# A gated cross-attention and ternary feed-forward kernel: 16-bit projections in a new order on every engine

## The reference

```python
q = heads(layernorm(x) @ Wq); k = heads(context @ Wk); v = heads(context @ Wv)
attn = softmax(where(mask, q @ k.T * 16 ** -0.5, -max))
x = x + tanh(g_xattn) * (merge(attn @ v) @ Wo)
h = gelu(layernorm(x) @ ternary(W1).T + b1)
x = x + tanh(g_ffn) * (h @ ternary(W2).T + b2)
```

## Time and profile before

| | |
|---|---|
| median of 3 runs | 1667.67 us (1663.63 to 1668.81) |
| profiled execution | 1664.17 us, its span 1662.4 us |
| busy in the span | PE 91%, DVE 90%, ACT 57%, POOL 40% |
| the chain that ended last | PE 55%, DVE 26%, issue 13%, ACT 3% |
| granted TensorE clock, mean | 0.984 of full |

### The profile page before, as it was taken

How to read it: one execution, slowest core, us unless ns; L and a number is a source line. 1 busy time by engine, 2 the same in 40 slices (tenths; PEclk the granted TensorE clock), 3 DMA queues, 4 the chain that set the end, 5 groups by cost and what they waited for, 6 DMA issues and landing times.

```text
span 1662.4 us, 48262 instructions
## 1 busy us (share of the span) xinstructions
PE 1508.0 (91%) x14501; PEld 1007.7 (61%) x14501; DVE 1489.1 (90%) x4379; ACT 939.8 (57%) x1799; POOL 668.8 (40%) x813
## 2 busy tenths in 40 slices
PE   3899999999999999999999999987999999999998
PEld 2566666666666666666666666655666666666665
DVE  7799999999999999999999999987888888888886
ACT  2456666665656666565656566654555555555554
POOL 5354555455555545554555545552111111111111
PEclk9899999999999999999999999996999999999999
DMA  2333333333333333333333333321010110101101
GB/s 78 92 99 85 96 84 88 93 86 97 84 96 83 97 84 94 86 87 95 86 97 83 98 83 95 81 49 55 26 38 25 38 38 25 38 25 38 38 25 51
DMA packets 207471, 117.93 MB, mean 71 GB/s; under 512 B 24912, under 2 KB 207184, under 8 KB 207440
## 3 DMA queue, kind: packets, MB, share of 16 engines
q1 hardware_dynamic: 207440, 117.54, 26.2%
HBM read 32.53 MB, written 16.78 MB: 30 GB/s over the span
## 4 chain that ended last, share of the span: by engine, by line
PE 55%; DVE 26%; issue 13%; ACT 3%; DVEq 2%; ACTq 0%; DMA 0%
PE bank L1069 12%; PE bank L312 9%; PE bank L1098 5%; PE bank L1099 5%; DVE smax L751 5%; PE bank L336 5%; PE bank L319 4%; PE bank L303 4%; DVE rstd L691 3%; DVE xres L796 3%; DVE k L721 3%; PE bank L392 2%; DVE rstd L693 2%; DVE y L1056 2%; DVE rstd L684 2%
## 5 line engine op out<-in xcount | busy, mean ns | idle before, releaser
L924 POOL TENSOR_TENSOR probl<-prob 128x512 f16<-128x512 f32 x512 | 529.2, 1042 | 531.2 <-ACT prob L602 530.3
L602 ACT ACTIVATE prob<-bank,masks 128x512 f32<-128x512 f32 x512 | 345.4, 688 | 138.9 <-PE bank L371 138.9
L751 DVE TENSOR_REDUCE smax<-bank 128x4 f32<-128x512 f32 x512 | 348.2, 681 | 13.5 <-PE bank L336 9.7
L1085 DVE TENSOR_TENSOR hidl<-hid 128x512 f16<-128x512 f32 x256 | 226.0, 883 | 80.5 <-ACT hid L1080 79.7
L1080 ACT ACTIVATE hid<-bank,b_sb 128x512 f32<-128x512 f32 x256 | 176.1, 688 | 211.3 <-PE bank L1069 205.3
L1069 PE MATMUL bank<-y,w1T 128*128 128x512 f16 x1024 | 264.6, 381 | 29.2 <-DVE y L1056 28.0
L1163 POOL TENSOR_TENSOR xres<-xres,b2g 128x1024 f32 (+1 forms) x32 | 75.7, 2366 | 431.4 <-ACT yln L1033 413.5
L1098 PE MATMUL bank<-w2T,hid 128*128 128x256 f16 x1024 | 237.4, 273 | 0.6 <-ACT w2T L1013 0.6
L1099 PE MATMUL bank<-w2T,hidl 128*128 128x256 f16 x1024 | 237.4, 273 | 0.0
L336 PE MATMUL bank<-k_rows,q_rows 64*128 64x128 f16 x2048 | 226.8, 220 | 5.6 <-DMA q_rows<-smaxT 3.4
L371 PE MATMUL bank<-q_rows,k_rows 64*128 64x128 f16 x2048 | 201.7, 219 | 0.8 <-DMA q_rows<-smaxT 0.8
(11 more groups left out here) (92 smaller groups left out, 2555.7 us busy)
## 6 DMA issues: line engine op xcount, KB each, us to landing
q_rows<-q SPq DMA_DIRECT2D x512, 64.0 KB, 2.5
k_rows<-k SPq DMA_DIRECT2D x512, 64.0 KB, 2.5
xres<-in_x_dram SPq DMA_DIRECT2D x64, 256.0 KB, 2.7
out_dram<-ystage SPq DMA_DIRECT2D x32, 512.0 KB, 2.9
ctx_sb<-in_ctx_dram SPq DMA_DIRECT2D x64, 192.0 KB, 3.2
q_rows<-smaxT SPq DMA_DIRECT2D x128, 8.0 KB
w_raw<-in_L_ffn_W_dram SPq DMA_DIRECT2D x2, 1024.0 KB, 7.0
prob<-in_L_xattn_Wq_dram SPq DMA_DIRECT2D x1, 256.0 KB, 4.2
```

Source lines behind the costliest of these rows:

```text
L602: act.activation(prob[u][:], st_bank[u % 2][:], ACT.Exp, bias=0.0, scale=masks[g.parity][:, 2 + b:3 + b]).then_inc(exp_done, 1)
L751: dve.tensor_reduce(smax[:, b, u * UH:(u + 1) * UH], sm_bank[u % 2][:].rearrange("p (h j) -> p h j", h=UH), AX.X, ALU.max).then_inc(max_ta ...
L924: pool.tensor_tensor(probl[u][:], prob[u][:], prob[u][:].bitcast(BF16)[:, 1::2], ALU.subtract).then_inc(prob_split, 1)
```

## The change

It has six parts.

1. The four weight matrices are scaled by 64 and split into two float16 parts at the start (ACT's `high_weights`, DVE's `low_weights`). Each float32 matmul of a projection becomes three 16-bit ones: high by high, high by low, low by high (`SPLIT`). The scale is taken off where q and k are split, through the gate for the output, and through the constant `vone` for v.
2. `xln` and the context are split before they are transposed. POOL's `low_x` and `low_ctx` write the float16 rest into the lower half of each float32 word in place, and PE transposes both halves as 16-bit tiles (8 transposes of 128x128 in place of 4, for each of the two). `low_prob` writes in place, too: `probl` is gone, and the low part is read with a step of two.
3. The attention result of both batches is transposed at once (4 float32 transposes), split (ACT `copy_attnT`, DVE `low_attn`), projected at once (12 matmuls) and added at once (one `add_attention` of 128x512).
4. The layer norm's statistics are taken once for four batches. In the loop DVE does only the first four parts (`seed_x`), and the Newton steps go to POOL (`root_x`, 14 parts over seven units). `load_x` loads four batches at once.
5. `read_weighed` writes its sums back to PSUM, from where `normalise` reads them. `low_q` and `low_k` are one instruction of 128x512 each, and k has two buffers.
6. All five lists are in a new order. The rough scores run one unit further ahead.

```diff
         def project_q(pe, g, m):
...
             for k in range(KD):
-                last = pe.matmul(pj_bank[:, m * T:(m + 1) * T], wq_sb[:, k, m * P:(m + 1) * P],
-                                 xlnT[:, k, :], start=(k == 0), stop=(k == KD - 1))
+                for i, (wp, xp) in enumerate(SPLIT):
+                    last = pe.matmul(by_batch(m), wq16[:, wp, k, m * P:(m + 1) * P],
+                                     typed(xT16[:, xp, k, :], xp).rearrange("p (b s) -> p b s", b=2),
...
         def read_weighed(dve, n, b, half):
...
-            dve.tensor_reduce(attn[b][:, heads, :],
-                              pv[:, :, 0:2 * HD].rearrange("p h (two d) -> p h d two", two=2), AX.X,
-                              ALU.add).then_inc(norm_read, 1)
+            dve.tensor_reduce(sums_of(half), pv[:, :, 0:2 * HD].rearrange("p h (two d) -> p h d two", two=2), AX.X,
+                              ALU.add).then_inc(sums_taken, 1)
...
-            dve.tensor_tensor(attn[b][:, heads, :], attn[b][:, heads, :],
+            dve.tensor_tensor(attn[b][:, heads, :], sums_of(half),
                               rsum[:, b, heads].unsqueeze(2).to_broadcast([P, HB, HD]),
...
+        def low_x(pool, g):
+            pool.wait_ge(ln_done, 2 * (g.n + 1))
+            x = xln[:].rearrange("p b d -> p (b d)")
+            pool.tensor_tensor(x.bitcast(F16)[:, 0::2], x, x.bitcast(BF16)[:, 1::2], ALU.subtract).then_inc(x_split, 1)
...
+        def low_attn(dve, g):
+            dve.wait_ge(attnT_high, g.n + 1)
+            dve.tensor_tensor(attnT16[:, 1].rearrange("p k t -> p (k t)"), tr_bank[:],
+                              attnT16[:, 0].rearrange("p k t -> p (k t)"), ALU.subtract).then_inc(attnT_split, 1)
...
         def low_prob(pool, g, b, u):
...
-            pool.tensor_tensor(probl[u][:], prob[u][:], prob[u][:].bitcast(BF16)[:, 1::2],
+            pool.tensor_tensor(prob[u][:].bitcast(F16)[:, 0::2], prob[u][:], prob[u][:].bitcast(BF16)[:, 1::2],
                                ALU.subtract).then_inc(prob_split, 1)
...
         def pool_group(pool, g, left):
             for b in range(2):
                 for u in range(UNITS):
                     low_prob(pool, g, b, u)
-                    if b == 1 and u == 0 and left >= 1:
+                    k = b * UNITS + u
+                    if g.parity == 1 and left >= 6 and k >= 4:
+                        for i in range(2 * k - 8, 2 * k - 6):
+                            root_x(pool, g.half + 3, i)
+                    if g.parity == 0 and left >= 4 and k < 3:
+                        for i in range(2 * k + 8, 2 * k + 10):
+                            root_x(pool, g.half + 2, i)
+                    if k == 3 and left >= 3:
+                        low_x(pool, g.after(3))
+                    if k == 4 and left >= 1:
                         pick_masks(pool, g.after(1))
+                    if k == 6 and left >= 3:
+                        low_ctx(pool, g.after(3))
```

More of the change, by code:

```diff
@@ L451, in pe_first @@
             transpose_max(pe, g0, 0, tr)
-            for u in range(2):
+            for u in range(3):
                 rough_scores(pe, g0, 1, u)
@@ L694, in ln_part @@
             else:
[L695 removed]
+                last = dve.scalar_tensor_tensor(norm[:, 0, :] if i == LN_PARTS - 2 else y, t, 1.5, y, ALU.add,
+                                                ALU.mult)
             last.then_inc(step, 1)
@@ new lines, in seed_x @@
+        def seed_x(dve, half, i):
+            past = half - 2
+            if i == 0:
+                dve.wait_ge(x_in, 16 * (half + 1))
+                for b in range(QB):
+                    last = dve.bn_stats(stats[:, b, :], row_of(half * QB + b))
+            elif i == 1:
+                if not (isinstance(half, int) and half == 2):
+                    dve.wait_ge(ln_ready, half)
+                dve.wait_ge(seed_step, past * (SEED_PARTS - 1) + 1)
+                dve.tensor_copy(rstd[:, 2, :], stats[:, :, 1])
+                for b in range(QB):
+                    last = dve.bn_aggr(meanvar[:, b, :], stats[:, b, :])
+            elif i == 2:
+                dve.wait_ge(seed_step, past * (SEED_PARTS - 1) + 2)
+                dve.tensor_scalar(newton[:, 2, :], meanvar[:, :, 1], EPS, -0.5, ALU.add, ALU.mult)
+                last = dve.tensor_scalar(newton[:, 0, :], meanvar[:, :, 1], EPS, None, ALU.add)
+            else:
+                dve.wait_ge(seed_step, past * (SEED_PARTS - 1) + 3)
+                dve.tensor_scalar(newton[:, 1, :].bitcast(I32), newton[:, 0, :].bitcast(I32), -0.5, RSQRT_SEED,
+                                  ALU.mult, ALU.add).then_inc(root_seeded, 1)
+                return
+            last.then_inc(seed_step, 1)
@@ L865, in dve_group @@
+                if g.parity == 1 and left >= 6 and i < SEED_PARTS:
+                    seed_x(dve, g.half + 3, i)
+            before = g.after(-1)
+            if not first:
+                read_weighed(dve, g.batch(0) - 1, 1, 0)
+                norm(0)
+                normalise(dve, before, 1, 0)
+            else:
+                norm(0)
             take_max(dve, g, 1, 3)
             round_max(dve, g, 1)
-            norm(10)
+            norm(1)
             low_max(dve, g, 1)
+            norm(2)
@@ L878, in dve_group @@
-            norm(13)
-            if left >= 1:
-                take_max(dve, g1, 0, 1)
-            read_weighed(dve, g.batch(0), 0, 0)
-            normalise(dve, g.batch(0), 0, 0)
+                norm(5)
+                normalise(dve, before, 1, 1)
+            else:
+                norm(5)
             if left >= 1:
                 take_max(dve, g1, 0, 2)
-            if left >= 2:
-                low_k(dve, g2)
-            if not first:
-                add_attention(dve, g.batch(0) - 1)
+            norm(6)
@@ L1020, in norm_y @@
             for i in parts:
-                if i == 3 and not (isinstance(g.half, int) and g.n == 0):
-                    dve.wait_ge(y_done, QB * g.n)
-                rows = [row_of(g.n * QB + b) for b in range(QB)] if i == 0 else (None,) * QB
+                if i == LN_PARTS - 2:
+                    if isinstance(g.half, int) and g.n == 0:
+                        dve.wait_ge(ln_done, B)
+                    else:
+                        dve.wait_ge(y_done, QB * g.n)
+                rows = [row_of(g.n * QB + b) for b in range(QB)] if i == 0 else ()
                 ln_part(dve, i, rows, y_step, g.n * (LN_PARTS - 1), y_ready)
@@ L1238, in _ @@
             pick_masks(pool, Group(0, 0))
-            over_groups(pool, pool_group)
+            low_x(pool, Group(0, 1))
+            low_ctx(pool, Group(1, 0))
+            low_x(pool, Group(1, 0))
+            for i in range(8):
+                root_x(pool, 2, i)
+            over_groups(pool, pool_group, 3)
             pool.wait_ge(b2_scaled, 1)
```

558 lines of the change are left out of this document (333 added, 225 removed).

## The result

The changed kernel takes 1804.91 us (median of 4 runs, 1793.73 to 1817.8), against 1667.27 us of the kernel before on the same chip (1663.63 to 1668.81): a ratio of 1.083 with the interval 1.075 to 1.092. It is slower by 8%. The forecast was 1513 us, its range ended at 1620, and "slower" had 0.08. The profiled execution took 1798.67 us, with a span of 1796.9 and a mean granted clock of 0.907 (before: 1664.17, 1662.4 and 0.984).

A forecast was written before the change was run, and what follows sets the result against it. PE and DVE were both taken as close to their limit. DVE's sum falls from 16.93 to 14.55 us a group, so 63.5 periods save 151 us of 1664.17: 1513 us, range 1435 to 1620.

The forecast's parts named there:

- slower: Outcome for the whole kernel: the change makes it slower than before; chance 0.08, beside faster 0.90 and same 0.02.
- DVE's part: DVE's sum per group in stage one: from 16.93 us, work and waits removed and added, to a period of 14.55.
- a chain and not DVE's work sets the period: Sign that the forecast is wrong: DVE idle for long behind POOL, SP or PE; no size or chance given.
- L939: On DVE, sign that the forecast holds: 0.29 us or less throughout, never 1.0.
- the 0.60 of `low_attn`: DVE's new split of the attention result adds 0.60 us a group, taken from L751's start-to-start time.
- Its term for such waits: DVE's small instructions waiting behind POOL: 5.5 candidates a group, 0.22 us each, +1.2 us.
- the seed's three: DVE's candidates for waits behind POOL in `seed_x`: a copy and two scalar operations for two groups, 0.22 us each.
- POOL: POOL's work per group goes from 8.9 to 12.7 us, 87% of 14.55; its in-place split taken as 1.02 us.
- PE: PE's work per group falls from 15.75 to 11.4 us, with 16-bit projections at 5.3 us in place of 9.6.
- The slower one: Rival: POOL never idles, DVE's small instructions wait a whole POOL instruction, 0.9 us each; period 18.3, 1751 us; chance 0.07.
- The clock: Rival: TensorE's clock falls to 1.2 GHz in a tenth of the groups, 0.8 us more on average; 1564 us; chance 0.04.
- SP's path of 13.7 us: SP's moves of k and the maximum's transfer until the next group's scores can start: 13.7 us, hidden under 14.55.

The follow-up runs named there:

- run 2: The changed kernel with twelve small filler matmuls on PE ahead of each of its four long waits in a group: 1750.84 us, ratio 1.052.
- run 18: Run 17's kernel with SP moving the maxima before k's four transfers and the seed's parts later on DVE: 1565.01 us, ratio 0.940.
- run 9: The changed kernel without the float16 rest of the rounded maxima (L914 on DVE, twice a group): 1683.94 us, ratio 1.013.
- run 16: The changed kernel with the seed in DVE's gaps and the rest of the rounded maxima on POOL as two instructions: 1726.69 us, ratio 1.036.
- Run 17: The changed kernel with PE, ACT and DVE lists in the old order, attention result per batch, POOL's split of `xln` earlier: 1678.14 us, ratio 1.0073.
- run 5: The changed kernel with DVE's `low_q` and `add_attention` moved behind other work: 1802.75 us, ratio 1.083.
- run 8: The changed kernel with `low_q` and `add_attention` later on DVE, second maxima transpose later on PE, `low_x` earlier on POOL: 1783.51 us, ratio 1.072.
- run 1: The kernel before, old order, each float32 projection matmul replaced by three 16-bit ones on upper halves, low parts left out: 1622.75 us, ratio 0.975.
- run 14: Run 1's kernel with the layer norm's Newton steps given from DVE to POOL: 1584.63 us, ratio 0.951.
- run 15: Run 1's kernel with all of the loop's layer norm left out but its last instruction, nothing given to POOL: 1506.80 us, ratio 0.904.
- run 3: The changed kernel with POOL's split of `prob` over half the elements: 1734.19 us, ratio 1.042.

## Why the prediction was wrong

**The step that failed** is the first line of DVE's part: the sum starts "from 16.93 us a group (its short idle waits stay in)". It takes for granted that what DVE loses in work the period loses too, and that the idle time stays as it was. That held before, where DVE idled for under 1 us a group. With work taken off PE and DVE and the lists rewritten, DVE's idle time went from under 1 to over 5 us, and at the full clock the loop took 18.22 us a group (run 2), where the sum had 14.55. The prediction named this sign itself ("a chain and not DVE's work sets the period") but had no rival for it. It never walked the new lists round from PE to DVE and back to see how long a round takes.

**The terms of DVE's sum were nearly right.** L939 takes 290 ns throughout, as forecast; L843's record of 678 ns less 0.08 is the 0.60 of `low_attn`; L948 takes 0.67 against 0.62. L914 and L907 take 567 and 267 ns, which is (0.39 + 0.09) x 2 = 0.96 us a group over calm records of 0.175. That is 0.24 each, where the prediction took 0.22. Its term for such waits was 1.2, of which the seed's three are 0.3. DVE's busy time is 573.09 / 800 x 19.02 = 13.6 us a group in the changed kernel and 13.7 in run 18, below the 14.55 that counted its gaps as well. Run 18 has groups of 14.2 us and a mean of 15.38. Its 1565 us are 52 above the forecast: the forecast was nearer to what this work can do in an order that feeds DVE, and said nothing of the order at hand.

**POOL**: 1043 ns for the split in place with a step of two, as taken. Busy for 494.22 of 800 us, 11.75 us a group, against 12.7; of the longer period that is 62% and not 87%.

**PE**: 12.8 us a group at the full clock in place of 11.4, 1.4 too low. The spacing of the 16-bit matmuls was as said (12 in 1.49 us, the last one's length included); from their starts to the next instruction's, the projections of the group shown take 5.7 us, against 5.3. Where the other 1.0 lies is open.

**The rivals.** The slower one (DVE's small instructions wait a whole POOL instruction each) gave 1751 and was wrong in its size: L914 lost 0.39 and not 0.9, and DVE was not full. But its place was right, for L914 turned out to be worth 121 us (run 9). It costs mostly because PE stands for it (run 16), not because it fills DVE. The clock had 0.04 and was priced at a tenth of the groups; it fell in nearly all of them and cost about 51 us (run 2), 0.80 us a group. The prediction's price was 0.8 us too, but that is luck: it had a tenth of the groups at half the clock throughout, and measured were 45 of 49 at a mean of mostly 0.75 to 0.95. PE's share had gone down to 76% in waits of 0.4 to 2.7 us, and the prediction counted PE's falling share as gain alone.

**SP.** The prediction hid SP's path of 13.7 us under the period of 14.55. In the changed kernel it stayed hidden. Run 17 shows what such a sum misses all the same: one transfer that PE waits for stood behind four that nobody waited for yet, and moving it ahead, together with a later seed, was worth 113 us (run 18).

## What to carry to other kernels

Before a sum of work is turned into a period, look at the idle time of the engine it is made for, and follow one round of the new lists: when a change takes work off the engines that were full, the period can pass from a sum to a loop. Then an instruction of 0.57 us that another engine waits for was worth 121 us (run 9), and the removal of waits of 2.4 us a group elsewhere nothing (run 5). Change the arithmetic and the order apart; here the new arithmetic took 1805, 1678 and 1565 us in three orders (the first with the joint result), against 1667 before. In each issuing queue, put what is waited for next ahead of what is only early.

## What the runs showed of the hardware

- The granted clock fell to half in the middle of a kernel that kept PE busy for 76 to 80%. It fell behind a stretch in which PE waited for DVE (busy for 1.26 of 4 us, with one wait of 2.74), and the next 4 us ran at 0.50 with PE busy for 3.89. The mean clock does not follow the length of the rounds: it was 0.907 in the changed kernel, 0.872 in run 8, where rounds of 16.53 us stand beside some of 21.19, and 0.963 in run 9, where the two shown take 16.33 and 17.52.
- A POOL split that writes every second 16-bit place of its own input takes 1043 ns, and the one to a tile apart 1042 (L924 in the page of before).
- DVE's waits behind POOL grow with what POOL does, and are counted as busy: the same product took 504 ns in run 1, 856 when POOL took over the Newton steps (run 14), and 562 when they were left out (run 15). A DVE instruction of 128x16 that starts beside a POOL split ends with it: 1.01 us beside one of 1.04, and 0.58 beside one of 0.62 (run 3).
